# A rotation ahead of three transformer layers: packed skew weights, exponentials of two batches side by side, and a QR in two halves

## What is computed

```python
def _rotation(cond, W, b):
    v = silu(cond) @ W.T + b                 # 2016 numbers for each batch
    A = zeros((B, 64, 64))
    A = A.at[:, iu, ju].set(v).at[:, ju, iu].set(-v)
    return expm(A)                           # one 64 x 64 rotation for each batch
```

## Time and profile before

| what | us |
|---|---|
| median of 3 runs (449.86 to 451.69) | 450.28 |
| the profiled execution | 449.79 |
| its span, first to last instruction | 448.0 |
| PE busy | 386.4 (86%) |
| DVE busy | 333.3 (74%) |
| ACT busy | 239.5 (53%) |
| POOL busy | 187.4 (42%) |
| mean granted TensorE clock | 0.851 of full speed |

### The profile page before, as it was taken

How to read it: one execution, slowest core, us unless ns; L and a number is a source line. 1 busy time by engine, 2 the same in 40 slices (tenths; PEclk the granted TensorE clock), 3 DMA queues, 4 the chain that set the end, 5 groups by cost and what they waited for, 6 DMA issues and landing times.

```text
span 448.0 us, 11399 instructions
## 1 busy us (share of the span) xinstructions
PE 386.4 (86%) x3762; PEld 278.4 (62%) x3762; DVE 333.3 (74%) x1578; ACT 239.5 (53%) x491; POOL 187.4 (42%) x576
## 2 busy tenths in 40 slices
PE   1099989999998866979999999999998989899746
PEld 0089977133895633647777776777676666667534
DVE  2899999999994435585877786777898989887120
ACT  1051010621235133466887978797787878786631
POOL 7435433344643612044354353534364636351340
PEclk9999995555555555696999999999999999999988
DMA  5445600000088000000000000000000000000000
GB/s 202 153 149 160 194 2 1 0 1 2 4 158 230 2 1 0 1 3 2 1 2 1 3 2 1 3 2 2 1 3 3 2 2 1 2 16 1 15 13 15
DMA packets 9499, 15.23 MB, mean 34 GB/s; under 512 B 1329, under 2 KB 7892, under 8 KB 9297
## 3 DMA queue, kind: packets, MB, share of 16 engines
q1 hardware_dynamic: 9442, 14.51, 11.3%
HBM read 13.88 MB, written 0.62 MB: 32 GB/s over the span
## 4 chain that ended last, share of the span: by engine, by line
PE 50%; DVE 15%; issue 11%; POOL 9%; ACT 9%; DMA 4%; SPq 1%; POOLq 0%; ACTq 0%; DVEq 0%
PE ps L775 42%; DVE nmax L1392 5%; DMA skw_r<-in_skw 4%; PE ps L978 4%; ACT skw_r L659 2%; PE ps L1035 2%; ACT brief L620 2%; ACT L651 1%; DVE st L1304 1%; POOL x L485 1%; PE ps L926 1%; ACT skw_t L634 1%; POOL tailp L460 1%; POOL tailp L458 1%; POOL tail L457 1%
## 5 line engine op out<-in xcount | busy, mean ns | idle before, releaser
L1392 DVE TENSOR_REDUCE nmax<-ps 128x4 f32<-128x512 f32 x96 | 62.6, 684 | 31.9 <-PE ps L775 31.8
L634 ACT ACTIVATE skw_t<-ps 128x512 f32<-128x512 f32 x96 | 53.4, 595 | 21.1 <-PE ps L775 20.8
L398 POOL TENSOR_TENSOR root<-grow,half 32x1 f32<-32x1 f32 x64 | 34.5, 539 | 70.2 <-DVE grow L1175 70.2
L775 PE MATMUL ps<-skw_r 54*128 54x128 bf16 x768 | 48.1, 223 | 5.9 <-DVE nmax L1392 4.0
L775 PEld LDWEIGHTS ps<-skw_r 54*128 54x128 bf16 x768 | 29.9, 96 | 27.3 <-issue 18.7
L775 PE MATMUL ps<-mT_t,fc1w_t 128*128 128x256 f32 x120 | 39.4, 420 | 1.4 <-ACT mT_t L672 1.3
L470 POOL TENSOR_TENSOR rstd<-vare,nhalf 128x1 f32<-128x1 f32 x24 | 13.3, 553 | 63.4 <-DVE vare L1310 46.8
L775 PE MATMUL ps<-fc2w,skw_r 128*128 128x144 f32 (+1 forms) x240 | 34.2, 290 | 0.6 <-ACT skw_r L659 0.6
L627 ACT ACTIVATE skw_r<-ps 128x512 bf16<-128x512 bf16 x48 | 26.1, 594 | 14.8 <-PE ps L978 14.4
L775 PE MATMUL ps<-s_t,skw_t 128*128 128x8 f32 x64 | 19.0, 371 | 16.9 <-DMA skw_r<-in_skw 16.9
L978 PE MATMUL ps<-identb,brief 128*128 128x128 bf16 x384 | 28.7, 234 | 4.9 <-DVE brief L1379 4.7
(11 more groups left out here) (222 smaller groups left out, 980.3 us busy)
## 6 DMA issues: line engine op xcount, KB each, us to landing
gmod<-spread_mods SPq DMA_DIRECT2D x3, 1408.0 KB, 9.2
skw_t<-in_skw SPq DMA_DIRECT2D x1, 2048.0 KB
adaw_t<-in_ada SPq DMA_DIRECT2D x3, 432.0 KB
tails<-in_tail SPq DMA_DIRECT2D x3, 427.1 KB
fc1w_t<-in_fc SPq DMA_DIRECT2D x3, 320.0 KB
fc2w<-in_fc SPq DMA_DIRECT2D x3, 288.0 KB
qkvw_t<-in_qkv SPq DMA_DIRECT2D x3, 216.0 KB
x<-in_x SPq DMA_DIRECT2D x1, 576.0 KB, 9.2
```

Source lines behind the costliest of these rows:

```text
L398: g.tensor_tensor(root[:, j:j + 1], grow[:, j % 4, j:j + 1], half[:], ALU.pow).then_inc(root_ready, 1)
L634: a.activation(prob[g].rearrange("p i t -> p (i t)"), ps[:, 2 + g % 2, :], ACT.Exp, scale=SCALE).then_inc(prob_ready, 1)
L775: return pe.matmul(o, lhsT, rhs, start=start, stop=stop, skip_group_check=True)
L1392: d.tensor_reduce(nmax[:, v % 2, first:first + 7:2], ps[:, 6 + g % 2, :].rearrange("p (i t) -> p i t", i=4), AX_X, ALU.max, negate=True).t ...
```

## The change

1. **Skew weights packed.** The strict upper triangle of A is folded into 32 x 64 numbers: the top left block with the transposed bottom right block below its diagonal, and the top right block. `skw_t` has 128 x 2048 numbers, and the 17 remaining rows of seven column blocks are stacked on 119 partitions (`skw_u`), with a block-diagonal moving tile `s_bd`. 64 products become 16 + 3. VectorE unfolds half of it with the masks `smask`, at step `LEAD_TAKES` of its first phase; `mods` packs its tails likewise.
2. **Two batches at once.** Batches 2b and 2b+1 lie on partitions 0 to 63 and 64 to 127 of every tile of the exponential; products come in pairs, each on its own quarter of the array. Fills have 256 columns instead of 512, and one `xp` takes the place of two.
3. **QR in two halves.** Phase A eliminates the leading 32 rows of the Gram matrix (`lead`). TensorE then makes the Schur complement and the first 32 columns of the top block (`lead_products`). Phase B eliminates 32 rows of both, side by side in one tile (`work`, 160 columns, 129 of them spread), with the sign found in the step itself. `work_products` makes the rest, and phase C does the last 32 x 32 top block (`last`). POOL's power is needed twice instead of 64 times, and `weight_left` no longer alternates with it.
4. **End of the rotation.** z = linvT^T xp and uT are made while phase C runs; after it the signs scale the exponential and uT, and y and the last product follow. ScalarE evacuates y.

```diff
-            for j in range(D):
-                pool.wait_ge(grow_ready, j + 1)
-                g.tensor_tensor(root[:, j:j + 1], grow[:, j % 4, j:j + 1], half[:], ALU.pow).then_inc(root_ready, 1)
-                if 10 <= j < 10 + 4 * LAYERS:
-                    weight_left(0, (j - 10) // 4, (j - 10) % 4)
-                elif 38 <= j < 38 + 8 * LAYERS and j % 2 == 0:
-                    weight_left(1, (j - 38) // 8, (j - 38) // 2 % 4)
...
+            root(0)
+            for l in range(LAYERS):
+                for c in range(4):
+                    weight_left(0, l, c)
+            for l in range(LAYERS):
+                for c in range(4):
+                    weight_left(1, l, c)
+            for l in range(LAYERS):
+                tail_mods(l)
+            root(1)
```

```diff
-                    for j in range(D // 2):
-                        mm(o[:, j * B:(j + 1) * B], skw_t[:, 2 * j * D:2 * (j + 1) * D], s_t[:], True, False)
-                        i = mm(o[:, j * B:(j + 1) * B], skw_u[:, 2 * j * D:2 * (j + 1) * D], s_u[:], False, True)
+                    for j in range(16):
+                        mm(o[:, j * B:(j + 1) * B], skw_t[:, 128 * j:128 * j + 128], s_t[:], j == 0, False)
+                    for g in range(3):
+                        n = min(PACK, 16 - PACK * g)
+                        i = mm(o[:, PACK * g * B:(PACK * g + n) * B], skw_u[:, g, :], s_bd[:, 0:n, :], False, g == 2)
...
                     if d < SQUARINGS:
...
                         for f in range(2):
-                            for b in range(B // 2):
-                                i = mm(o[:, f * (B // 2) + b, :], e[:, 1 - f, g * (B // 2) + b, :], e[:, f, g * (B // 2) + b, :])
+                            for b in range(2):
+                                for r in both_halves:
+                                    i = mm(o[r, f * 2 + b, :], e[r, 1 - f, 2 * g + b, :], e[r, f, 2 * g + b, :])
...
+                if (name, arg) == FIRST_HALF_AFTER:
+                    lead_products()
+                if (name, arg) == SECOND_HALF_AFTER:
+                    work_products()
...
+            pe.wait_ge(last_ready, 1)
+            for r in both_halves:
+                i = mm(ps[r, 6, :], linvT[r, :], xpT[r, :])
+            i.then_inc(zT_full, 1)
...
+            for n in range(2):
+                pe.wait_ge(rmi_ready, n + 1)
+                for b in range(2 * n, 2 * n + 2):
+                    for r in both_halves:
+                        i = mm(ps[r, n, (b % 2) * T:(b % 2 + 1) * T], rmi[r, b, :], zT[r, b * T:(b + 1) * T])
+                i.then_inc(y_full, 1)
```

`FIRST_HALF_AFTER` is ("n2", 0), `SECOND_HALF_AFTER` is ("square", (4, 1)). On VectorE, phase B (A and C are alike, with fewer instructions; A is the first row block below):

```diff
+            for j in range(HALF):
+                row, f = brow[:, j % 2, :], fac[:, j % 2, :]
+                e = slice(D + j + 1, 2 * D + j + 1)
+                need(upd)
+                need(spread(work[:, j:2 * D + j + 1], row[:, j:2 * D + j + 1], j))
+                need(did(d.scalar_tensor_tensor(out=row[:, j:j + 1], in0=row[:, j:j + 1], scalar=-0.5, in1=row[:, j:j + 1],
+                                                op0=ALU.is_ge, op1=ALU.add)))
+                need(did(d.reciprocal(brec[:, j, :], row[:, j:j + D + 1:D])))
...
+                    k_fac = did(d.scalar_tensor_tensor(out=f[:, 1:2], in0=work[:, D + j:D + j + 1], scalar=brec[:, j, 1:2],
+                                                       in1=below[:, j:j + 1], op0=ALU.mult, op1=ALU.mult))
+                k_fac2 = did(d.scalar_tensor_tensor(out=f[:, 0:1], in0=work[:, j:j + 1], scalar=brec[:, j, 0:1],
+                                                    in1=notj[:, j:j + 1], op0=ALU.mult, op1=ALU.mult))
+                if j < HALF - 1:
+                    need(k_fac)
+                    did(d.scalar_tensor_tensor(out=work[:, e], in0=row[:, e], scalar=f[:, 1:2], in1=work[:, e],
+                                               op0=ALU.mult, op1=ALU.add))
+                need(k_fac2)
+                i = d.scalar_tensor_tensor(out=work[:, j + 1:D], in0=row[:, j + 1:D], scalar=f[:, 0:1],
+                                           in1=work[:, j + 1:D], op0=ALU.mult, op1=ALU.add)
```

More of the change, by code:

```diff
@@ L77, in plan_rotation @@
     chain += [("square", (k, g)) for k in range(1, SQUARINGS) for g in (0, 1)] + [("square", (SQUARINGS, 0))]
-    other = [("mods", 0)] + [("gate", l) for l in range(LAYERS)] + [("xp", 0), ("xp", 1)]
+    other = [("mods", 0)] + [("gate", l) for l in range(LAYERS)] + [("xp", 0)]
     fills = chain[:2]
@@ L82, in plan_rotation @@
     return fills
+LEAD_TAKES = 24
+FIRST_HALF_AFTER = ("n2", 0)
+SECOND_HALF_AFTER = ("square", (4, 1))
 def head_of(g, i):
@@ L1270, in _ @@
             need(k)
[L1271 to L1272 removed]
+            k = did(d.tensor_tensor(picked[:, 0, :], arec[:], pick[:, 1, :], ALU.mult))
             need(k)
[L1274 to L1278 removed]
@@ new lines, in _ @@
+            k2 = did(d.tensor_copy(linvT[:], ps[:, 6, 0:D]))
+            need(k)
+            for at in (0, D):
+                d.scalar_tensor_tensor(out=s128[at:at + HALF, :], in0=sgn[:, 0:1], scalar=4.0, in1=rs[:, 0:1], op0=ALU.mult,
+                                       op1=ALU.mult)
+            dve.wait_ge(wp_full, 1)
+            need(k2)
+            d.tensor_tensor(zz[:], pT2[0:D, HALF:D], ps[0:D, 7, 0:HALF], ALU.subtract).then_inc(zz_ready, 1)
+            dve.wait_ge(last_full, 1)
@@ new lines, in _ @@
+            dve.wait_ge(rs_ready, 2)
+            d.scalar_tensor_tensor(out=last[:], in0=ps[0:HALF, 7, D:D + HALF], scalar=rs[:, 1:2], in1=nhalf_i[:, 0:HALF],
+                                   op0=ALU.mult, op1=ALU.add).then_inc(last_ready, 1)
+            dve.wait_ge(last_ready, 1)
+            upd = 0
+            for j in range(HALF):
+                row = crow[:, j % 2, :]
+                need(upd)
+                need(spread(last[:, j:HALF], row[:, j:HALF], j))
+                need(did(d.scalar_tensor_tensor(out=row[:, j:j + 1], in0=row[:, j:j + 1], scalar=-0.5, in1=row[:, j:j + 1],
+                                                op0=ALU.is_ge, op1=ALU.add)))
+                k = did(d.reciprocal(crec[:, j:j + 1], row[:, j:j + 1]))
+                need(k)
+                if j == HALF - 1:
+                    break
+                need(did(d.scalar_tensor_tensor(out=fac[:, j % 2, 0:1], in0=last[:, j:j + 1], scalar=crec[:, j:j + 1],
+                                                in1=below[:, j:j + 1], op0=ALU.mult, op1=ALU.mult)))
+                upd = did(d.scalar_tensor_tensor(out=last[:, j + 1:HALF], in0=row[:, j + 1:HALF], scalar=fac[:, j % 2, 0:1],
+                                                 in1=last[:, j + 1:HALF], op0=ALU.mult, op1=ALU.add))
@@ new lines, in _ @@
+            need(did(d.scalar_tensor_tensor(out=picked[:, 0, :], in0=crec[:], scalar=0.0, in1=pick[:, 0, :], op0=ALU.is_ge,
+                                            op1=ALU.mult)))
+            need(did(d.tensor_reduce(sgn[:, 0:1], picked[:, 0, :], AX_X, ALU.add)))
+            need(did(d.tensor_scalar(sgn[:, 1:2], sgn[:, 0:1], -0.5, 4.0, ALU.add, ALU.mult)))
+            for at in (HALF, D + HALF):
+                i = d.tensor_tensor(s128[at:at + HALF, :], sgn[:, 1:2], rs[:, 1:2], ALU.mult)
```

548 lines of the change are left out of this document (296 added, 252 removed).

## The result

The changed kernel takes 435.52 us (median of 4 runs, 434.48 to 437.08), the kernel before 450.07 (4 runs, 449.59 to 451.69): ratio 0.9674, 95% interval 0.9631 to 0.9716. The profiled execution took 434.67 us, its span is 432.8. It is faster by 15.1 us than the profiled one of before, where 8.5 were forecast. Executions that lie more than 1.5% above the fastest of their kernel are left out of all ratios and their intervals.

What follows compares the result with a forecast made beforehand. VectorE's elimination chain, with TensorE equally full beside it, was taken as the bound; first `x += rotation` 143.6 instead of 152.08 us, 8.5 earlier: 449.79 becomes 441.3, plus 0.49 for the median, 441.8 us; range 434 to 449.

Steps and rivals of the forecast that it cites:

- Price of a link, phase steps: VectorE's unoverlapped chain in phases A, B, C: 35 ns between instructions, steps 0.965, 1.425, 1.05 us, sum 108.3 us.
- the rival of 57 ns: VectorE's chain: 57 ns instead of 35 over 470 links, 10.4 us more, 452.2 us, slower; chance 0.06.
- The stall: Phase B: POOL's 24 tail-weight additions hold up VectorE instructions with two SBUF tensors, 0.69 us each, 16.5 us.
- The bounds, 0 and 23.8: Phase B: nothing lost if all additions fall beside shuffle or reciprocal; 24 x 0.99 = 23.8 us at most.
- TensorE at nothing: TensorE until the end of phase B: its work costs no time, VectorE's chain covers it.
- at most 95: TensorE finishes `square (4,1)` by 95 us, before phase B ends at 103.7 us.
- Pairs overlap: After phase C: two y product pairs on opposite array quarters, 0.92 us if overlapping; rival without overlap 1.5 us more, 0.15.
- The tail: After phase C: about 1.25 us of VectorE work, then y, evacuation, last product and hand-overs, together 3.6 us.
- B to C: Passage between phases B and C: vector links, two products and hand-overs, 2.4 us.
- The layers: Three transformer layers after the rotation, code untouched: they last 296 us as before.

Runs made afterwards that it cites:

- e1: Changed kernel with POOL's 24 additions to the tail weights left out, so part of these weights is wrong: 423.33 us.
- e12: Changed kernel with POOL's first 12 tail-weight additions started behind the shuffle of step 2 of phase B: 432.72 us.
- e2: Changed kernel with POOL's first 12 tail-weight additions issued ahead of the first root, so that they run in phase A: 430.83 us.
- e4: Changed kernel with the squarings of levels 1 to 4 issued four times over, same result: 436.89 us.
- e11: Changed kernel with the squarings of levels 1 to 4 issued ten times over: median of ten executions 452.7 us, ratio to the kernel before 0.9997.
- e8: The kernel before, unchanged, profiled once more: span 451.3 us, first `x += rotation` on VectorE at 155.41 us.
- e9: The kernel before with three squarings in place of seven, which gives another exponential: 445.09 us, ratio 0.9896.
- e3: Changed kernel with the eight y products reordered, the four of the lower array quarter first, the four of the upper behind them: 437.89 us.
- e10: The changed kernel, unchanged, measured and profiled once more: 434.68 us.
- e5: Changed kernel with the tail-weight additions moved from POOL to VectorE, as six inside phases A and B: 431.12 us.
- e6: Changed kernel with 23 extra TensorE products in phase C, into a bank that nobody reads: 435.23 us.
- e7: Changed kernel with tail-weight additions on VectorE, two inside the elimination and four in VectorE's waits: 426.64 us, ratio 0.942.

## Why the prediction was right, and where it was not

*The sign and the mechanism* were right: VectorE's chain is the bound of the changed kernel, its steps cost what was forecast, TensorE lost its place on the path. The size was too small: 441.8 us were forecast, 435.52 measured. That is inside the stated range (434 to 449), 1.5 us from its edge, and just outside the forecast's own 437.5 to 446. Of the miss, 4.1 us are a stall priced too high and 3.4 a gain of the layers that the prediction had no term for; the other terms took 0.85 back. A gain without a term was not covered by the range, so that the range held is in part luck. By steps:

- *Price of a link, phase steps.* Forecast 0.965, 1.425 and 1.05 us. Measured 0.99, 1.43 to 1.46 and 1.03 to 1.10. A ended at 40.0 (39.4), B began at 41.76 (41.8), C ran 33.6 us (33.05 and 0.7 for POOL's small instructions were forecast; no step of C was longer beside them). The 35 ns of the earlier trace rows carry over: the links of the new chain show 30 to 40; the rival of 57 ns is out. (The prediction's own terms add up to 39.5 for the end of A and 143.5 for the first add, 0.1 off what it writes.)
- *The stall*, "0.69 each, 16.5 us", is the term that was mis-sized: 12.4 us, 7.44 for the first 12 and 5.0 for the second, which e1 confirms. The bounds, 0 and 23.8, held it. The step failed where it said that each addition costs VectorE 0.69 us: in the second batch VectorE's shuffle, reciprocal and the useful length of the blocked instruction itself run beside the additions, so 12 additions of 8.5 us cost 5.0. It also held that "a blocked instruction can lose no more than the 0.74 us of one addition"; one instruction was held for 7.59 us, across eleven of them. e12 and e2 show that the same twelve cost 7.44, 5.0 or 3.5 us by where they stand. The page "SBUF — State Buffer" of the Trainium skill (section "SBUF: two separate sides") calls the port pair an exclusive lock for the whole instruction; the prediction's estimate from it, 17.8 us, is 5.4 too much, since an addition costs nothing while VectorE does not ask for the ports. The trace agrees with the lock itself: the blocked instruction of 7.59 us ends at 49.67 us, the additions at 49.66.
- *TensorE at nothing* was right for the changed kernel: wait of 24.7 us, e4 without effect, e11 with the cliff where the slack ends. The forecast "at most 95" was far on the safe side (75.5): the squarings ran in pairs, and the clock was at 1.00 from 54.0 to 71.0 and 74.4 to 77.8 us. What was incomplete is the picture of before: e8 and e9 show that TensorE's chain came last there, so TensorE's cut is worth 4.1 us by itself against the first profile and 7.4 against the second; the ratio of e9, over executions of before of both kinds, gives 1.0%.
- *Pairs overlap*: 0.92 us forecast for two pairs; 1.97 were measured for four, of which the first two took 1.12, and e3 shows the overlap by order alone. The rule that speaks against it (the Trainium skill, "TensorEngine Tiling (Array Packing)", "Gotcha 1: PSUM Pressure": different row tiles cannot access one PSUM bank at the same time) does not hold for these quarters: they write different partitions of one bank and run side by side.
- *The tail* took 4.25 us from the end of C, 3.6 were forecast, mostly for the products: 0.2 more for the first two pairs of y, and 0.97 us from the start of the last product to the first add, where 0.55 and a hand-over had been put; *B to C* 2.15 in place of 2.4.
- *The layers, "296 us as now"*, is the second step that missed: 292.55, 3.4 us of gain that no term had. The stall's 4.1 and the layers' 3.4 less the tail's 0.65 and 0.2 of the other terms are the 6.6 us between forecast (441.3) and profile.

Over fourteen profiles the layers' length goes with the clock. Where every window of 10 us from 180 to 400 us had 1.00, the layers took 292.4 to 292.6 us (after, e2, e4, e10, e12) or 290.7 (e1); where a window between 180 and 210 us had 0.66 to 0.80, they took 294.0 to 295.9 (before, e3, e5, e6, e7, e8, e9, e11). The traces place the loss. Two instructions of VectorE, the same pair in both kernels, after and then before:

```profile
190.53 0.46 DVE L1485 TENSOR_TENSOR brief<-res,brief 128x288 bf16<-128x288 f32 x1
194.08 0.69 DVE L1498 TENSOR_REDUCE nmax<-ps 128x4 f32<-128x512 f32 x1 [0.85 <-PE ps L823]
```

```profile
203.25 0.46 DVE L1379 TENSOR_TENSOR brief<-res,brief 128x288 bf16<-128x288 f32 x1
209.74 0.69 DVE L1392 TENSOR_REDUCE nmax<-ps 128x4 f32<-128x512 f32 x1 [1.90 <-PE ps L775]
```

They lie 3.55 us apart after and 6.49 before, because VectorE waits longer for TensorE: this is where the clock of before is at 0.50 for 6.8 us. Between 50 and 60 us behind the first add all eight profiles with a relapse lose 2.7 to 3.0 us against the changed kernel, the other five lose nothing there, and behind it no difference changes by more than 0.2 us over the next 180 us. Before lost another 0.9 us at its fall at 181 us. So the clock's part is shown, but not what starts a relapse: e6 kept the array at work ahead of the layers and had one, e7 moved two additions, e3 changed the order of eight products, and both had one, the changed kernel had none in two profiles. Of the 15.1 us, 11.8 are earned before the first add, and 3.4 come with the clock, of which no run here says that another edit would keep them.

## What to carry to other kernels

Price an exclusive lock by what the other engine would do in that time, not by the number of blocking instructions: the same work cost 12.4 us on POOL beside VectorE's bare chain, 6.8 as six instructions of the chain itself, and what was put into waits cost the first add nothing. When each instruction of an engine waits for the one before it, look for the waits of the same engine a little later, and put the side work there. And where two engines run nearly full until the same moment, take a second profile before saying which is the bound: before had executions of two kinds, 2.7 us apart.

## What was not expected of the hardware

- One VectorE instruction on a single column was held for 7.59 us by twelve additions of POOL of 0.71 us each; started two steps later the same additions let VectorE in after each one. The hold came back within 0.01 us in all six profiles with this order.
- The PEclk column can read 1.00 where no clock was recorded. In 120 to 130 us of before the rows are

```profile
120.00:130.00 10.00, 10.00 (x97) 10.00 (x96) 9.54 (x69) 3.55 (x6) 4.67 (x9) 0.50 0.52 103
```

in the first profile, and in the second

```profile
120.00:130.00 10.00, 9.53 (x90) 9.56 (x91) 9.54 (x68) 3.28 (x6) 4.88 (x10) 1.00 0.59 115
```

with the same 3.62 us for thirty-two records of a squaring in both. The clock records of the second trace begin at 181.0 us, those of the first at 61.6, and ahead of the first record the column reads 1.00 in each. The length of the products says more: two records of 128x8 take 0.59 us at 23 to 57 us of the first profile, with nothing recorded, and 0.39 at 63 us, where 1.00 is recorded; at the same product the second profile has 0.59. So the second kind of before is most likely the one whose clock did not rise at n2, and the means of 0.977 and 0.851 are both too high, since they count unrecorded time as 1.00. Where the clock is recorded, products follow it: with four times the squarings (e4) a hundred and twenty-eight records, in pairs, take 3.95 us at 69.6 us, where the clock is 1.00, and thirty-two take 1.97 at 102 us, after a wait and at 0.50, twice as long for each.
